# Routing of two batch rows inside the attention groups, and activation transposes in halves

## The reference

```python
x = x + tanh(g_xattn[0]) * xattn0(layernorm(x), ctx)   # 16 heads, time bias, softmax
x = x + tanh(g_ffn[0])   * ffn0(layernorm(x))          # ternary weights, relu
x = x + tanh(g_xattn[1]) * xattn1(layernorm(x), ctx)   # 16 heads of 16, relu projections
x = x + tanh(g_ffn[1])   * ffn1(layernorm(x))          # four experts
```

```python
logits = x @ W_router
expert_idx = argmax(logits, -1)
h = gelu(einsum('th,ehi->tei', x, W1) + b1)            # 256 -> 1024 for each expert
intermediate = einsum('te,tei->ti', one_hot(expert_idx), h)
y = intermediate @ Wo + bo + x                          # 1024 -> 256
y = layer_norm(y) * gamma + beta
```

## Time and profile before

| what | value |
|---|---|
| median of 3 runs | 829.76 us (828.74 to 833.25) |
| the profiled execution | 835.91 us |
| its span, first to last instruction | 834.1 us |
| mean granted TensorE clock in it | 0.925 |
| PE (TensorE) busy | 737.3 us, 88% |
| DVE (VectorE) busy | 581.4 us, 70% |
| ACT (ScalarE) busy | 440.8 us, 53% |
| POOL (GpSimd) busy | 296.2 us, 36% |

### The profile page before, as it was taken

One profiled execution on the slowest core, in us unless ns is written; L12 is line 12 of the kernel. 1 busy time (PEld: TensorE's weight loads), 2 busy tenths in 40 slices (PEclk: granted clock), 3 DMA queues, 4 the chain that ended last, 5 costly groups with the idle time before them and its releaser, 6 DMA issues.

```text
span 834.1 us, 12041 instructions
## 1 busy us (share of the span) xinstructions
PE 737.3 (88%) x4096; PEld 428.6 (51%) x4096; DVE 581.4 (70%) x1126; ACT 440.8 (53%) x840; POOL 296.2 (36%) x348
## 2 busy tenths in 40 slices
PE   5897599999998998999768999899999886899991
PEld 3443234343432676777523334333353775799981
DVE  5473689999970489265758899799943537577775
ACT  2222488888887535665016888687853422233330
POOL 2121255555554234755000000755423304233322
PEclk9897699999999999999877999999975989899996
DMA  8497355454444431002722255522012202111100
GB/s 298 112 180 219 108 179 180 169 170 155 166 166 155 152 101 51 1 1 73 173 62 81 71 175 169 149 77 64 18 46 83 92 1 90 39 48 44 42 15 21
DMA packets 51357, 87.52 MB, mean 105 GB/s; under 512 B 8598, under 2 KB 16792, under 8 KB 51297
## 3 DMA queue, kind: packets, MB, share of 16 engines
q1 hardware_dynamic: 44320, 72.06, 28.2%
q0 software_dynamic: 4576, 11.54, 5.3%
q10 hardware_dynamic: 2400, 3.15, 1.1%
HBM read 45.29 MB, written 41.63 MB: 104 GB/s over the span
## 4 chain that ended last, share of the span: by engine, by line
PE 56%; issue 11%; DVE 11%; DMA 8%; POOL 6%; SPq 4%; ACT 3%; POOLq 0%; DVEq 0%; ACTq 0%
PE ps_out L712 14%; PE ps_a L698 10%; PE ps_wide L593 6%; DVE row_max L1395 5%; PE ps_misc L698 5%; PE ps_a L522 4%; DMA out_x<-sorted_rows,ids 3%; PE ps_a L830 3%; SPq L438 2%; PE ps_wide L688 2%; POOL sorted_rows L1287 2%; PE ps_wide L894 1%; POOL hid_lo L1255 1%; PE ps_out L844 1%; ACT probs L1020 1%
## 5 line engine op out<-in xcount | busy, mean ns | idle before, releaser
L1395 DVE TENSOR_REDUCE row_max<-ps_wide 128x2 f32<-128x1024 f32 x256 | 301.1, 1219 | 34.0 <-PE ps_wide L593 27.8
L1020 ACT ACTIVATE probs<-ps_a 128x512 f32<-128x512 f32 x342 | 191.5, 602 | 57.4 <-PE ps_a L698 49.4
L593 PE MATMUL ps_wide<-stack_k,stack_q 48*128 48x512 f32 x512 | 155.1, 472 | 15.2 <-DVE row_max L1395 11.0
L698 PE MATMUL ps_a<-stack_q,stack_k 62*128 62x512 f32 (+1 forms) x342 | 142.3, 467 | 13.1 <-ACT probs L1020 10.1
L712 PE MATMUL ps_out<-probs,vals 128*17 128x512 f32 x1024 | 142.2, 631 | 0.5 <-POOL probs L1214 0.5
L698 PEld LDWEIGHTS ps_a<-stack_q,stack_k 62*128 62x128 f32 (+1 forms) x342 | 61.9, 194 | 102.4 <-ACT probs L1020 69.3
L1020 ACT ACTIVATE probs<-ps_misc 128x512 f32<-128x512 f32 x170 | 102.4, 603 | 19.4 <-PE ps_misc L698 15.5
L1214 POOL TENSOR_TENSOR probs<-probs,fixes_sb 128x512 f32<-128x512 f32 x64 | 82.2, 1284 | 82.5 <-ACT probs L1020 82.5
L593 PEld LDWEIGHTS ps_wide<-stack_k,stack_q 48*128 48x128 f32 x512 | 63.0, 191 | 50.5 <-DVE row_max L1395 20.2
L698 PE MATMUL ps_misc<-stack_q,stack_k 62*128 62x512 f32 (+1 forms) x170 | 78.8, 463 | 2.9 <-ACT probs L1020 2.9
L1199 POOL TENSOR_SCALAR max_neg<-row_max 128x16 f32<-128x16 f32 x32 | 9.2, 289 | 158.5 <-DVE row_max L1395 137.3
(11 more groups left out here) (214 smaller groups left out, 1326.7 us busy)
## 6 DMA issues: line engine op xcount, KB each, us to landing
rows_sorted<-blank SPq DMA_DIRECT2D x17, 1040.0 KB, 5.0
planes_k<-planes SPq DMA_DIRECT2D x32, 256.0 KB, 3.8
planes_q<-planes SPq DMA_DIRECT2D x32, 256.0 KB, 3.5
stack_q<-planes_q SPq DMA_DIRECT2D x64, 128.0 KB, 2.8
stack_k<-planes_k SPq DMA_DIRECT2D x64, 128.0 KB, 2.8
w_raw<-in_L_W SPq DMA_DIRECT2D x6, 1024.0 KB, 5.1
stack_q<-planes_q SPq DMA_DIRECT2D x64, 64.0 KB, 2.7
stack_k<-planes_k SPq DMA_DIRECT2D x64, 64.0 KB, 2.6
```

Of the source, the lines that this page charges most:

```text
L593: mm(raw_slot(l, ("pair", g, p))[:, i * S:(i + 1) * S], stack_q[at, slot(g, c) + q * P:slot(g, c) + (q + 1) * P], stack_k[at, slot(g, c):s ...
L698: mm(score_slot(("tile", n))[:], stack_k[at, slot(g, c) + k * P:slot(g, c) + (k + 1) * P], stack_q[at, slot(g, c):slot(g, c) + S], start=T ...
L1020: do(probs[n % PROBS[l]][:, j, :], score_slot(("tile", n * HG + j))[:], ACT.Exp, scale=0.25).then_inc(exp_done, 1)
L1395: v.tensor_reduce(row_max[:, g % 2, :, p], raw_slot(l, ("pair", g, p))[:].rearrange("p (i k) -> p i k", i=2), AX, ALU.max).then_inc(sem(f" ...
```

## The change

Routing of batch rows 0 and 1 moves forward in attention 1, by the group number g of each engine's loop. On TensorE `turn_n3(0)` and `route_logits(0)` go to group 11 (steps 2 and 3), `count(0)` to group 12 (step 0), `turn_n3(1)` and `route_logits(1)` to group 13, `count(1)` and `total(0)` to group 14 (step 0). On VectorE `update3` of tiles 4 and 5 and `normal(3, 0)` follow the maxima for group 12, `route(0)` and `update3` of tiles 6 and 7 those for group 13, `place(0)` stands inside those for group 14, `normal(3, 1)` behind them and `route(1)` behind those for group 15. GpSimd sends the rows of batch row 0 inside attention, and the first two gathers wait for the scores of group 13 only. Behind attention each step of routing rows 2 and 3 moves by up to a block, and the roots of blocks 0 to 2 are issued ahead of the gathers of phase 1. `turn_hidden(n)` is split: four transposes after the first half of `down(n - 1)`, four after the second.

```diff
@@ raw_items: the order in which items take the two double banks
-                if l == 1 and g == G + 1:
-                    for what, b in (("n3", 0), ("n3", 1), ("logits", 0), ("count", 0), ("logits", 1), ("count", 1)):
-                        yield (what, b)
+                if l == 1 and g == G - 2:
+                    yield ("logits", 0)
+                if l == 1 and g == G:
+                    yield ("logits", 1)
+                    yield ("count", 1)
                 for p in range(PAIRS):
+                    if l == 1 and (g, p) in ((G - 3, 6), (G - 1, 6)):
+                        yield ("n3", (g - G + 3) // 2)
+                    if l == 1 and (g, p) == (G - 2, 2):
+                        yield ("count", 0)
@@ TensorE, the expert blocks
-            turn_n3(2)
-            route_logits(2)
             turn_rows(0)
+            turn_n3(2)
...
                 if n == 0:
+                    route_logits(2)
+                if n == 1:
                     count(2)
                     turn_n3(3)
-                if n == 1:
+                if n == 2:
                     route_logits(3)
-                if n > 0:
-                    down(n - 1)
-                turn_hidden(n)
-                if n == 1:
+                for half in range(2):
+                    if n > 0:
+                        down(n - 1, range(half * FC // 2, (half + 1) * FC // 2))
+                    turn_hidden(n, (half,))
+                if n == 2:
                     count(3)
                     total(1)
@@ GpSimd, behind attention
-            roots(3, 1)
-            pool.wait_ge(sem("rows_cleared"), 16 * (G + 1))
-            place_rows(0)
             place_rows(1)
             roots(3, 2)
-            for n in range(2):
+            for n in range(FIRST):
                 gather(n)
             roots(3, 3)
-            for n in range(2, FIRST):
-                gather(n)
-            place_rows(2)
-            place_rows(3)
-            for n in range(3):
-                gather(FIRST + n)
-            for n in range(2):
-                root4(n)
-            for n in range(2, BLOCKS + 2):
-                if n < BLOCKS:
-                    root4(n)
-                scatter(n - 2)
-                m = n + ROW_RING - 2
-                if FIRST + 3 <= m < BLOCKS:
-                    gather(m)
+            place_rows(2)
+            root4(0)
+            root4(1)
+            place_rows(3)
+            root4(2)
+            for n in range(FIRST, FIRST + 2):
+                gather(n)
+            for n in range(3, BLOCKS):
+                root4(n)
+                scatter(n - 3)
+                if n + 4 < BLOCKS:
+                    gather(n + 4)
+            for n in range(BLOCKS - 3, BLOCKS):
+                scatter(n)
@@ VectorE, the expert blocks
+            rows_low(0)
             for t in tiles(3, None):
                 update3(t)
             aggregate(3, 3, 1e-5)
+            rows_low(1)
             route(2)
-            rows_low(0)
             normal(3, 3, x)
-            rows_low(1)
-            place(2)
             hidden_low(0)
             for n in range(1, BLOCKS + 1):
+                if n == 3:
+                    place(3)
+                    tables(1)
                 if n + 1 < BLOCKS and n != FIRST - 1:
                     rows_low(n + 1)
+                if n == 1:
+                    place(2)
                 if n == BLOCKS:
                     finish(n - 2)
                 residual(n - 1)
+                if n == 2:
+                    route(3)
                 if n < BLOCKS:
                     hidden_low(n)
-                if n == 1:
-                    route(3)
-                if n == 2:
-                    place(3)
-                    tables(1)
```

More of the change, by code:

```diff
@@ L741, in attention @@
                                 turn_out(g - BEHIND)
-                        if l == 1 and (g, k) == (G - 2, 1):
-                            turn_n3(0)
                 for n in range(G * QT - BEHIND, G * QT):
@@ L1029, in attention @@
                                 keep_out(g - 1)
-                            if l == 1 and j == 0 and g == G - 2 and k - 2 in range(EARLY_ROWS):
-                                if k == 2:
-                                    act.wait_ge(sem("b1_split"), 1)
-                                rows1(k - 2)
+                            if l == 1 and (g, k, j) == (G - 5, 3, 0):
+                                act.wait_ge(sem("b1_split"), 1)
+                                rows1(0)
+                            if l == 1 and (g, k, j) == (G - 3, 3, 0):
+                                rows1(1)
                             weights(g, k, j)
@@ L1165, in expert_weights, with number_rows, place_rows @@
                 halves(w1_hi[:, e, cols], w1_lo[:, e, cols], w1_raw1[:, e, cols], QT * e + q)
+            def number_rows():
+                pool.wait_ge(sem("w_last"), 16 * 7)
+                v.tensor_copy(rows_all[:, :, 2 * D:ROW], table[:, TOKENS:STEPS].unsqueeze(2).broadcast_to([P, T, ROW - 2 * D])
+                              ).then_inc(sem("numbered"), 1)
+                pool.wait_ge(sem("numbered"), 1)
+            def place_rows(b):
+                pool.wait_ge(sem("dest_ready"), b + 1)
+                for t in range(b * QT, (b + 1) * QT):
+                    nc.gpsimd.indirect_dma_start(rows_sorted, bass.IndirectOffsetOnAxis(dest[:, t:t + 1], 0), rows_all[:, t, :], None
+                                                 ).then_inc(sem("rows_sent"), 16)
             def hidden_weights():
@@ L1224, in attention @@
                         roots(3, 0)
+                    if l == 1 and g == G - 4:
+                        roots(3, 1)
                     if l == 1 and g == G - 3:
+                        pool.wait_ge(sem("rows_cleared"), 16 * (G + 1))
+                        number_rows()
+                        place_rows(0)
                         hidden_weights()
@@ L1266, in _ @@
             attention(1)
-            def place_rows(b):
-                pool.wait_ge(sem("dest_ready"), b + 1)
-                for t in range(b * QT, (b + 1) * QT):
-                    nc.gpsimd.indirect_dma_start(rows_sorted, bass.IndirectOffsetOnAxis(dest[:, t:t + 1], 0), rows_all[:, t, :], None
-                                                 ).then_inc(sem("rows_sent"), 16)
             def gather(n):
-                if n == 0:
-                    pool.wait_ge(sem("scores_done1"), QT * B * H)
+                if n in (0, 2):
+                    pool.wait_ge(sem("scores_done1"), QT * HG * (G - 2 if n == 0 else G))
                 if n in (0, FIRST):
@@ L1524, in attention @@
                             normalise(g - BEHIND - 2)
+                        if l == 1 and (g, p) == (G - 2, 2):
+                            place(0)
                         if g < G:
                             maximum(l, g, p)
-                    if l == 1 and g >= GB + BEHIND + 2:
+                    if l == 1 and GB + BEHIND + 2 <= g < G - 4:
                         update3(g - GB - BEHIND - 2)
-                        if g % GB == GB - 1:
-                            aggregate(3, (g - GB - BEHIND - 2) // GB, 1e-5)
+                    if l == 1 and g == G - 5:
+                        aggregate(3, 0, 1e-5)
+                    if l == 1 and g == G - 4:
+                        update3(4)
+                        update3(5)
+                        normal(3, 0, x)
+                    if l == 1 and g == G - 3:
+                        route(0)
+                        update3(6)
+                        update3(7)
+                        aggregate(3, 1, 1e-5)
+                    if l == 1 and g == G - 2:
+                        normal(3, 1, x)
+                    if l == 1 and g == G - 1:
+                        route(1)
                 if l == 1:
-                    normal(3, 0, x)
-                    normal(3, 1, x)
+                    place(1)
                     normalise(G - 4)
-                    route(0)
-                    place(0)
-                    for t in tiles(2, None)[0:2]:
+                    for t in tiles(2, None):
                         update3(t)
-                    route(1)
-                    place(1)
-                    for t in tiles(2, None)[2:4]:
-                        update3(t)
-                    normalise(G - 3)
                     aggregate(3, 2, 1e-5)
                     tables(0)
+                    normalise(G - 3)
                     normal(3, 2, x)
@@ L1742, in _ @@
                 residual(n - 1)
+                if n == 2:
+                    route(3)
                 if n < BLOCKS:
                     hidden_low(n)
-                if n == 1:
-                    route(3)
-                if n == 2:
-                    place(3)
-                    tables(1)
                 if n == 3:
                     finish(0)
-                if n > 2 and n < BLOCKS:
+                if n == 4:
+                    finish(1)
```

(1 more changed line is left out.)

23 lines of the change are left out of this document (11 added, 12 removed).

## The result

The changed kernel took 840.13 us (median of 3; 836.54 to 842.59) against 829.76 (828.74 to 833.25): a ratio of 1.0095, 95% interval 1.0048 to 1.0141, slower. In six more executions beside 23 of the kernel before it was 847.79 against 831.37 us, 1.0194 [1.0125, 1.0263]. The forecast was 834.0, its range 819 to 841.

A forecast was written before the change was run, and what follows sets the result against it. Bounds: TensorE and VectorE with little slack in attention, half clock in groups 14 and 15, then the blocks behind VectorE's chain. Attention's end +12.7, behind it -9, tail +0.4: +4.1 us on the median, about 834; range 819 to 841.

The forecast's parts named there:

- The sign: Whole kernel: forecast slower, +4.1 us; chances put at slower 0.47, same 0.27, faster 0.26.
- (a): Attention groups 11 to 13: added routing work costs 13.4 us, plus 3.6 us of clock losses.
- the loss put at 3.6: Groups 11 to 13: three clock losses of 1.2 us each behind TensorE waits, bounds 0 and 7.
- Rival 2: Groups 11 to 13: engines overlap the added routing, costing near 7.0 us without clock losses; 824 us, chance 0.14.
- Rival 3: Low clock from count(0) lasts through groups 12 and 13, some eight steps; about +15, 845 us, chance 0.10.
- (b): Attention groups 14 and 15: clock falls in the first step and stays down; 40.9 us instead of 45.2, gaining 4.3.
- rival 1: Clock stays up in groups 14 and 15, which gain 17.7 us; sum -11.7, 818 us, chance 0.16.
- the reason given: Groups 14 and 15: logits, one thin step, then count preceded the clock's fall before and would again.
- (c): Behind attention: routing of rows 2 and 3 spread over blocks, block 5 resumes sooner; 9 us gained, bounds 4 and 11.
- (d): Blocks and tail: transposes in halves gain 0; one more scatter behind root4(18) at the end costs +0.4 us.
- the base: The +4.1 us, worked out on the profiled span of 834.1 us, was put on the median of 829.76.

The follow-up runs named there:

- again: The changed kernel itself, unaltered, executed six more times and profiled a second time (span 842.9 us): 847.8 us, ratio 1.0194 to before.
- burst: Kernel before plus one unused VectorE reduction of 2560 elements behind the maxima for group 12: 836.3 us, ratio 1.0063.
- narrow: Kernel before plus 16 products of 4 columns ahead of each of groups 12 and 13: 839.0 us, ratio 1.0064.
- smooth: Changed kernel with VectorE's added work in groups 12 to 14 put piece by piece between the maxima: 845.8 us, ratio 1.0178 to before.
- gather5: Changed kernel with each gather issued one block earlier: 838.3 us, ratio 1.0022 to before.
- inside: Kernel before with only the change's part in attention, old order behind attention: 847.0 us, ratio 1.0075.
- late5: "behind5" with routing of rows 0 and 1 two steps later in attention, VectorE's normalise of group 13 moved along: 827.0 us, ratio 0.9917 to before.
- behind5: Kernel before with only the change's part behind attention, and each gather one block earlier: 826.3 us, ratio 0.9927.
- whole5: "behind5" with the split of the hidden transposes undone, eight whole behind the down product: 827.2 us, ratio 0.9914 to before.
- behind5b: The same program as "behind5", run once more: 827.0 us, ratio 0.9938 to before.
- filler: Kernel before with two of four score products issued twice per step in groups 14 and 15 of attention 1: 833.1 us, ratio 0.9998.

## Why the prediction was right or wrong

The sign was right and the time inside the range, near its upper end. That was partly luck of the first three executions: the median of the six others, 847.79 us, lies outside it, and so does that of all nine, 842.6. The size, +4.1 against +10.4 and +16.4 us, was less than half of the real one, and the terms show where.

- **(a) groups 11 to 13.** From group 10's turn to the start of group 14 are 602.86 - 563.5 = 39.4 us before, 621.49 - 560.7 = 60.8 now and 619.81 - 561.6 = 58.2 in "again": +21.4 and +18.8, forecast 13.4 + 3.6 = 17.0. The terms without the clock came out: waits of 2.40 + 0.40 for 2.9, a turn, logits, 2.28 of wait and a count, 1.0 + 1.9 + 2.3 + 1.2 = 6.4, for 6.5 (turn and count at their full-clock prices, since here they ran at half clock), two waits of 0.75 and 0.40 near 610 us for 1.1, and 1.09 + 2.25 = 3.3 for 2.9; together 13.6. What is left is the clock's, by difference 7.8 and 5.2 us: the loss put at 3.6 was mis-sized, and in the first profile passed its bound of 7. The row it was sized by had 3.4 us at half clock behind a wait; the changed kernel had 9.8 and 10.0 us in two stretches, and the first of them was 3.4 in "again" behind the same wait of 2.40 us. "burst" gave 4.3 us for the wait with its clock step that was put at 4.1, "narrow" 1.7 for a set put at 1.9. Rival 2 is out: "smooth" found nothing to hide. Rival 3 came partly true: the low level went on behind count(0), for 5 us (one step and the turns behind it), not for eight steps.
- **(b) groups 14 and 15.** Forecast 40.9 us; "again" took 659.28 - 619.81 = 39.5, the first profile 31.6, since its clock rose halfway. The forecast describes one draw, and rival 1 is partly true in the other. The other profiles with this attention show both draws as well: from group 14's turn to T "gather5" took 20.9 us like the first profile, "inside" 28.8 like "again" (28.7). Both start with the fall that was forecast. "late5" fits the reason given (logits, one step, count) and does not prove it. What I had not seen is that one program draws either, so that one profile can't carry a sum to 1%. From group 10's turn, T moved by +7.8 and +13.1 us, forecast +12.7.
- **(c) behind attention.** Forecast 54.5 us from T to block 5's rows; 56.0 to 57.3 were measured, against 63.7 before: 6.4 to 7.7 us instead of 9.2. VectorE's chain behind tables(1) was 709.14 - 693.46 = 15.7 us, as worked out (15.2 to 16). But tables(1) ended at T + 40.3, not 38.5, and up(0) began at T + 4.5, not 3.8. The prediction also leaves out that the gather of block 5 now stands behind root4(2): TensorE waited 2.54 us for these rows at 703.66. It cost nothing here, since VectorE, busy until 708.66, came to their low part 4 us after ScalarE had the high part ready; a faster VectorE would meet it.
- **(d) the tail.** This step failed: "At the very end one more scatter stands behind root4(18) ... +0.4". The end itself did cost 0.5 us. But it overlooked that the change also issues every gather two roots later, gather(m) behind root4(m - 4) instead of root4(m - 6). Four blocks then wait for their rows; their periods are 8.03, 7.65, 7.80 and 7.76 us instead of 7.21, and the tail is 3.3 to 4.0 us longer. "gather5", "behind5" and "whole5" show that all but 0.5 to 0.8 us comes from the distance of the gather.

The measured terms add up: 7.8 - 7.7 + 3.3 = +3.4 us in the first profile and 13.1 - 6.4 + 4.0 = +10.7 in "again", less the 2.8 and 1.9 us by which these two reached group 10's turn sooner than before's profile did: +0.6 and +8.8, the differences of the spans. That head start belongs to the last error, the base: I set before's profiled 834.1 us, which I ascribed "to nothing in particular", equal to its median. The median span of 35 executions is 830.3, so "again" lies 12.6 us above it; the medians differ by 10.4 and 16.4. How much of that comes from the low stretches that the changed kernel's executions draw stays open.

The version to keep is the part behind attention with gathers one block earlier: 0.9927 [0.9892, 0.9962] and 0.9938 [0.9902, 0.9974]; without the split 0.9914 [0.9881, 0.9947], which the same intervals can't tell apart.

## What to carry to other kernels

Work moved into a stage where two engines already feed each other without slack cost nearly its full length here, on either engine, and cutting it up saved nothing; and what frees a thin stage returns only as far as the clock there allows. When an order of issues is rewritten, compare for each buffer how far ahead of its use the transfer is now issued; a loop that looks the same with one index changed can be a transfer that has become just too late. And where executions scatter by a per cent, compare stretches between fixed points of several profiles, and set the base by the median, not by the one that was profiled.

## What the runs showed of the hardware

- The same program draws different low stretches of TensorE's clock: groups 14 and 15 of the changed kernel took 31.6 or 39.5 us, and from group 14's turn to T the one program of "behind5" and "behind5b" took 40.0 or 37.4. Over "again", the mean clock was 0.925 at 841.17 us and 0.909 at 852.04.
- TensorE can be busy and still be granted half: 21.8 of 22.6 us in "behind5b", at a clock of 0.50.
- A fall comes a few us behind narrow products or an idle of 2.2 to 2.4 us, but not behind each: one set of 16 products was followed by 6.8 us at 1.2 GHz, the same set 15.5 us later by none. After the idle it was 3.4 us in "burst" and "again" and 9.8 in the first profile of the changed kernel.
- 16 products of 4 columns take 1.95 us, 8 of 512 columns by 17 rows 1.05; and giving a thin step two products more ("filler") didn't keep the clock up: it was low for some 20 us of groups 14 and 15.
